# Token-major attention outputs, a dense output projection, a reordered opening and stacks copied on chip

## Chip, cores and metric

The kernel runs on one core of a Trainium2 chip. The metric is the device time of one execution, in microseconds, lower is better. The engines are named PE (TensorE), DVE (VectorE), ACT (ScalarE), POOL (GpSimd) and SP (SyncE, which here only issues DMAs). Each has its own in-order stream of instructions; they meet at semaphores that the program places by hand.

## What is computed

One transformer layer over 4 batches of 256 tokens with width 256, all in float32. Cut to what matters:

```python
h = layernorm(x)
q, k, v = rope(h @ Wq.T), rope(h @ Wk.T), h @ Wv.T          # then 16 heads of 16
kf, qf = elu(k) + 1, elu(q) + 1
mem_out = (qf @ (kf.T @ v)) / (qf @ kf.sum(tokens))         # linear attention
attn = softmax(q @ k.T / 4) @ v
g = sigmoid(gate)                                            # one number a head
x = x + (g * mem_out + (1 - g) * attn) @ Wo.T
u = layernorm(x)
x = x + fwht(silu(u @ W1.T) * (u @ W3.T)) @ W2.T             # fwht: Walsh-Hadamard over 1024
```

The transform fwht is applied once to W2 instead of to every token. W1 and W3 are 256 to 1024, W2 is 1024 to 256.

## The kernel before

**Precision.** Projections and the FFN split each operand into a high part (type F32R) and a low remainder, and add three products (hi-hi, hi-lo, lo-hi). `three` (L848 to L850), `ffn_up` (L1010, L1014) and `ffn_down` (L1032, L1036) do that.

**Attention scores.** For each head `q_stack` and `k_stack` (128 rows, one slot a head) hold three slots of 16 rows: q is (hi, lo, hi), k is (hi, hi, lo), so one matmul over all rows gives the split product. Rows 64 and 65 of q hold the negated row maximum (hi and lo), and those of k hold ones. So PE first computes all 16 heads' scores (`scores`, L901), DVE takes the row maxima (`row_maxima`, L628), the maxima are transposed, negated and sent by two small DMAs into rows 64 and 65 of `q_stack`, and PE computes the scores a second time, shifted and transposed (`shifted_scores`, L919). ACT takes the exponential (`exp_head`, L367), and `product_v` (L936) multiplies with v.

**Filling the stacks.** RoPE works on [feature, token] tiles: `rope_product` (DVE, L639), sums (`first_rope_sum`, L644, on DVE for batch 0; `rope_sums`, L506, on POOL after that), high part on ACT (`split_parts`, L325), low part (`first_low_part`, L649, DVE; `low_parts`, L513, POOL). SP writes the parts to a DRAM scratch `parts` (`write_parts`, L261), waits for that, and reads them back into the stacks (`load_stacks`, L274): for each half c of the heads six DMAs of 128 KB, each into 16 rows. For batches after the first they start when the shifted scores of the old half are done. The unused rows of both stacks are zeroed by POOL at the start (L490, L534, L536).

**Attention outputs before.** `product_v` leaves 4 heads at a time as [head strip of 32 rows, token], with the softmax denominator in row 16 of each strip. `read_memory` (L969) gives the linear part in the same layout. DVE's `weights` (L696 to L711) turns the denominators with 32x32 transposes, takes the reciprocal, multiplies by the gate and turns them back; `combine` (L720, L723) scales and adds. It is called in three pieces per batch: pieces 0 and 1 at the end of the batch's round, piece 2 early in the next round after head 2's row maxima. POOL's `norm_linear` (L531) scales the linear part. `project_out` (L988) then contracts the 128 strip rows of each of 4 groups with a `wo` that is half zeros, on top of the residual that `residual_in` (L979) brought in through the identity. `evac_x2` (ACT, L379) copies the sum to `xs`.

**Order of the work.** A prologue computes batch 0's q, k, v. Then rounds r = 0 to 4 are written out by hand for each engine. In round r PE computes the scores of batch r (16 heads), among them q, k, v of batch r + 1 and the output projection of batch r - 1; then 16 steps of shifted scores of batch r, among them the FFN chunks of batch r - 1 (8 chunks) and `product_v`. In every one of these steps h, PE takes what is listed for h in order, and a wait there holds all that comes later. The weight transform is done in between: `hadamard` (PE, L1046, in the prologue and at heads 6 and 7 of round 0), `butterfly` (L233; step 0 on POOL, steps 1 and 2 on DVE), `split_w2` and its low part. The low parts of W1 and W3 are two POOL instructions at L542.

**SP's queue** at the start: x of batch 0, Wq, Wk, x of batch 1, W1, W3; then, once the q, k, v weights are split, W2, x of batches 2 and 3, Wo. The DMAs of one queue are served in order.

## Time and profile before

| | us |
|---|---|
| median of 3 runs | 251.93 |
| lowest, highest | 249.94, 252.1 |
| the profiled execution, its own time | 254.45 |
| its span, first to last instruction | 252.6 |
| mean granted TensorE clock | 0.932 of full |

The page gives busy time by engine; the timeline gives start and duration of instructions, with the idle time before them and what ended it in brackets. A release by DMA means that the landing of that transfer was waited for.

### The profile page before, as it was taken

What the parts mean: (1) busy time and instruction counts of PE and PEld (TensorE: products, weight loads), DVE (VectorE), ACT (ScalarE), POOL (GpSimd) and SP (SyncE); (2) the same over time, 40 slices, a digit from 0 to 9 for tenths busy, and PEclk for the clock granted to TensorE, in tenths of its full rate; (3) what the DMA queues carried; (4) which work ended last, traced back from release to release, by engine and by line L of the source; (5) the groups of instructions that cost most, each with busy time, mean ns of one, the idle gap of its engine ahead of it and who ended that gap; (6) DMA issues with size and microseconds to landing.
All of it is one profiled execution on the core that took longest, in us unless ns stands there. A gap on an engine that the chain in (4) does not pass through costs nothing.

```text
span 252.6 us, 4048 instructions
## 1 busy us (share of the span) xinstructions
PE 200.2 (79%) x1444; PEld 169.1 (67%) x1444; DVE 174.9 (69%) x341; ACT 97.8 (39%) x196; POOL 95.7 (38%) x73
## 2 busy tenths in 40 slices
PE   0064066886897949999999699999879999959894
PEld 0064055873544939997788599877769986748893
DVE  6966862498898597838879967448998562962442
ACT  2261131042884012368810325686021577312231
POOL 7919500069450738323610492152021215111332
PEclk9999655799997997999999899999999999997999
DMA  6919299313087103002790130066800100000101
GB/s 217 384 29 260 86 176 120 38 43 130 0 122 114 22 31 111 31 2 51 79 128 1 43 114 20 4 91 99 109 0 0 49 0 3 1 1 0 44 0 42
DMA packets 16940, 17.67 MB, mean 70 GB/s; under 512 B 1676, under 2 KB 16268, under 8 KB 16908
## 3 DMA queue, kind: packets, MB, share of 16 engines
q1 hardware_dynamic: 16168, 16.68, 31.9%
q10 hardware_dynamic: 752, 0.73, 0.9%
q8 instruction: 11, 0.18, 0.4%
q14 instruction: 9, 0.07, 0.1%
HBM read 11.93 MB, written 5.24 MB: 68 GB/s over the span
## 4 chain that ended last, share of the span: by engine, by line
PE 43%; issue 22%; DVE 17%; POOL 8%; DMA 6%; SPq 2%; ACT 2%; POOLq 0%; DVEq 0%; ACTq 0%
DVE rowmax_pad L628 5%; DMA k_stack<-parts 5%; PE score_bank L901 5%; PE score_bank L1010 4%; PE exp_bank L919 4%; DVE xn L611 4%; PE down_bank L1032 4%; POOL hid_lo L525 4%; PE exp_bank L1010 3%; PE misc_bank L848 2%; DVE prod L639 2%; PE pv_bank L936 2%; PE misc_bank L849 2%; PE misc_bank L850 2%; PE misc_bank L969 2%
## 5 line engine op out<-in xcount | busy, mean ns | idle before, releaser
L628 DVE TENSOR_REDUCE rowmax_pad<-score_bank 128x2 f32<-128x512 f32 x64 | 42.8, 685 | 17.8 <-PE score_bank L901 17.8
L525 POOL TENSOR_TENSOR hid_lo<-wide_raw,hid_hi 128x256 fp32r<-128x256 f32 x32 | 25.0, 782 | 70.6 <-ACT hid_hi L400 67.1
L367 ACT ACTIVATE prob<-exp_bank 128x512 f32<-128x512 f32 x64 | 37.8, 601 | 15.4 <-PE exp_bank L919 15.1
L901 PE MATMUL score_bank<-k_stack,q_stack 128*128 128x256 f32 x128 | 31.1, 337 | 14.7 <-DVE rowmax_pad L628 10.5
L901 PEld LDWEIGHTS score_bank<-k_stack,q_stack 128*128 128x128 f32 x128 | 21.8, 205 | 20.0 <-DVE rowmax_pad L628 10.8
L919 PE MATMUL exp_bank<-q_stack,k_stack 128*128 128x256 f32 x128 | 28.5, 306 | 2.5 <-DMA q_stack<-nmT_lo 1.4
L919 PEld LDWEIGHTS exp_bank<-q_stack,k_stack 128*128 128x128 f32 x128 | 19.2, 189 | 14.0 <-issue 8.2
L506 POOL TENSOR_TENSOR roped<-prod 128x512 f32<-128x512 f32 x6 | 7.6, 1271 | 44.0 <-DVE prod L639 44.0
L738 DVE SCALAR_TENSOR_TENSOR wide_raw<-wide_raw,score_bank 128x256 f32<-128x256 f32 x16 | 6.7, 418 | 23.3 <-ACT wide_raw L394 23.3
L861 PE MATMUL misc_bank<-cst,xn 128*128 128x128 f32 x16 | 3.4, 351 | 23.9 <-DVE xn L611 23.9
L1032 PE MATMUL down_bank<-w_hi,hid_hi 128*128 128x256 f32 x64 | 17.5, 296 | 1.4 <-ACT hid_hi L400 1.4
L861 PEld LDWEIGHTS misc_bank<-cst,xn 128*128 128x128 f32 x16 | 2.3, 178 | 24.1 <-issue 13.1
L988 PE MATMUL pv_bank<-wo,att 128*128 128x256 f32 x64 | 16.3, 382 | 1.7 <-DVE att L723 1.7
L611 DVE TENSOR_SCALAR xn<-xs,mv,rstd 128x256 f32<-128x256 f32 x16 | 12.3, 809 | 7.6 <-POOL rstd L499 7.3
L1010 PE MATMUL exp_bank<-h2T_hi,w_hi 128*128 128x256 f32 x64 | 17.4, 294 | 0.0
L1010 PE MATMUL exp_bank<-h2T_hi,w_lo 128*128 128x256 f32 x64 | 17.1, 288 | 0.0
L1010 PE MATMUL score_bank<-h2T_hi,w_hi 128*128 128x256 f32 x64 | 17.0, 289 | 0.0
L1032 PE MATMUL down_bank<-w_lo,hid_hi 128*128 128x256 f32 x64 | 16.5, 281 | 0.0
L1010 PE MATMUL score_bank<-h2T_hi,w_lo 128*128 128x256 f32 x64 | 16.4, 280 | 0.0
L379 ACT ACTIVATE xs<-pv_bank 128x512 f32<-128x512 f32 x4 | 2.4, 598 | 35.1 <-DVE stats L592 35.1
L325 ACT ACTIVATE part_hi<-roped 128x512 fp32r<-128x512 f32 x8 | 5.0, 630 | 27.8 <-POOL roped L506 20.3
L936 PE MATMUL pv_bank<-prob,v_strips 128*32 128x256 f32 x192 | 15.3, 391 | 0.1
(117 smaller groups left out, 547.4 us busy)
## 6 DMA issues: line engine op xcount, KB each, us to landing
q_stack<-parts SPq DMA_DIRECT2D x24, 128.0 KB
k_stack<-parts SPq DMA_DIRECT2D x24, 128.0 KB
parts<-part_hi SPq DMA_DIRECT2D x8, 256.0 KB, 2.2
parts<-part_lo SPq DMA_DIRECT2D x8, 256.0 KB, 2.4
xs<-in_x SPq DMA_DIRECT2D x4, 256.0 KB, 6.6
wide_raw<-in_w1T SPq DMA_DIRECT2D x1, 1024.0 KB, 8.2
wide_raw<-in_w3T SPq DMA_DIRECT2D x1, 1024.0 KB, 10.0
narrow_raw<-in_w2T SPq DMA_DIRECT2D x1, 1024.0 KB, 6.0
```

The lines of the kernel that those rows point to most:

```text
L367: act.activation(prob[:, h % 8], exp_bank[h % 2][:], ACT.Exp, scale=SCALE).then_inc(prob_s, 1)
L506: pool.tensor_tensor(roped[:, c], prod[:, 2 * c], prod[:, 2 * c + 1], (ALU.subtract, ALU.add)[c]).then_inc(rope_sum, 1)
L525: pool.tensor_tensor(hid_lo[:, n % 3, :], ffn_work[n % 3], hid_hi[:, n % 3, :].bitcast(F32), ALU.subtract).then_inc(hid_lo_s, 1)
L611: dve.tensor_scalar(xn[:, tt, :], xs[:, b, tt, :], mv[:, tt, 0:1], rstd[:, tt:tt + 1], ALU.subtract, ALU.mult).then_inc(ln_xn, 1)
L628: dve.tensor_reduce(rowmax[:, h, :], score_bank[h % 2][:], AX.X, ALU.max).then_inc(rowmax_s, 1)
L738: dve.scalar_tensor_tensor(out=work, in0=work, scalar=1.0, in1=chunk_bank(n)[:, 0, :], op0=ALU.add, op1=ALU.mult).then_inc(gated_s, 1)
L901: mm = pe.matmul(bank[:, tt, :], q_stack[:, h, tt * P:tt * P + P], k_stack[:, h, :], start=True, stop=True)
L919: mm = pe.matmul(bank[:, tt, :], k_stack[:, h, tt * P:tt * P + P], q_stack[:, h, :], start=True, stop=True)
L936: mm = pe.matmul(bank[STRIP * j:STRIP * j + STRIP, half, :], v_strips[b % 2][:, tt, h, :], prob[:, h % 8, tt, :], start=(tt == 0), stop=(t ...
L988: mm = pe.matmul(bank[:, tt, :], att[:, g, tt * P:tt * P + P], wo[:, g, :], start=False, stop=(g == NG - 1), skip_group_check=True)
L1010: pe.matmul(bank[:, m, :], w[:, m, k, cols], h2T_hi[:, k, :], start=(k == 0 and w is w13_hi), stop=False)
L1032: pe.matmul(bank[:, tt, :], hid_hi[:, n % 3, tt * P:tt * P + P], w[:, c, :], start=(c == 0 and tt == 0 and w is w2_hi), stop=False, skip_g ...
```

## The change

1. **Opening.** POOL no longer clears the stacks. It fills a small tile with zeros and ones, and SP issues three DMAs that copy it into the rows the scores need (48 to 65 of q, 48 to 63 and 64 to 65 of k) behind W1. The scores contract 66 rows instead of 128. W3, W2, x of batch 2, Wo, x of batch 3 are issued only behind batch 0's twelve stack copies. ACT splits W1 and W3 after the work of batch 0. The low parts of W1 and W3 are cut into four POOL instructions each; W3's stand in round 0 ahead of butterfly step 0. All four hadamards stand at heads 5 to 8 of round 0. Batch 1's layer norm is ahead of batch 0's RoPE.
2. **Stacks.** `write_parts` and the DRAM scratch go. The columns of Wq and Wk are reordered on the host so that a half's 128 rows are (dim, head), and `load_stacks` copies straight from `part_hi` and `part_lo` in SBUF: four copies when the high part is ready, two when the low part is.
3. **Outputs.** `product_v` writes two groups into `pv_bank`; ACT copies them (`evac_att`); PE transposes them to [token, strip] (`transpose_att`, 4 transposes); DVE's `combine` takes the reciprocal of the denominators (now a column), multiplies by the gate, scales and adds the linear part, which `linear_part` has scaled straight from PSUM; PE transposes the 128 combined columns back (`transpose_comb`, 2 transposes), ACT copies them (`evac_combT`), and `project_out` contracts 2 x 128 dense rows. The residual is added by DVE at the head of `ln_statistics`. `residual_in`, `evac_lin`, `evac_x2` and `norm_linear` go. `read_memory` now streams 136 columns instead of 256.

```diff
 load_stacks(b, c):
-                sp.wait_ge(parts_out[c], 32 * (b + 1))
                 if b == 0:
-                    sp.wait_ge(stack_zero, 2)
+                    sp.wait_ge(stack_zero, 48)
                 else:
                     sp.wait_ge(exp_ps, NH * (b - 1) + HH * (c + 1))
...
+                for src, ready, slots in ((part_hi, part_hi_s, ((0, 0), (0, 2), (1, 0), (1, 1))),
+                                          (part_lo, part_lo_s, ((0, 1), (1, 2)))):
+                    sp.wait_ge(ready, DC * b + c + 1)
+                    for m, s in slots:
+                        sp.dma_start((q_stack, k_stack)[m][HD * s:HD * s + HD, HH * c:HH * c + HH, :].bitcast(F32),
+                                     src[:, c, m, :].bitcast(F32)).then_inc(stack_in[c], 16)

+            def late_loads():
+                sp.dma_start(wide_raw[:, 1], w3T.rearrange("(c p) n -> p c n", p=P)).then_inc(w13_in[1], 16)
...
+                sp.dma_start(w2_raw, w2T.rearrange("(c p) n -> p c n", p=P)).then_inc(w2_in, 16)
+                sp.dma_start(xs[:, 2], xv(x, 2)).then_inc(x_in[2], 16)
+                sp.dma_start(wo[:], woT.rearrange("(c p) n -> p c n", p=P)).then_inc(wo_in, 16)
+                sp.dma_start(xs[:, 3], xv(x, 3)).then_inc(x_in[3], 16)

 POOL, round 0:
                 if has(r + 1):
                     low_parts(r + 1)
                 if r == 0:
+                    wide_low(1)
                     butterfly(pool, 0)

 DVE:
+            def combine(b, u):
+                n = 2 * b + u
+                strips = pv_bank[:].rearrange("p t (s e) -> p (t s) e", e=STRIP)
+                dve.wait_ge(attT_ps, n + 1)
...
+                dve.reciprocal(att_inv[:]..., strips[:, :, HD]).then_inc(att_inv_s, 1)
+                dve.tensor_tensor(att_wt[:], att_inv[:], gate2[...]..., ALU.mult).then_inc(att_wt_s, 1)
+                dve.tensor_tensor(att_n[:]..., strips[:, :, 0:HD], att_wt[:]..., ALU.mult).then_inc(att_n_s, 1)
...
+                dve.tensor_tensor(comb[:, :, cols], att_n[:], lin_n[:, :, cols], ALU.add).then_inc(comb_s, 1)

 DVE, end of a round:
                 if has(r):
                     combine(r, 0)
                 if has(r + 1):
-                    row_maxima(r + 1, (0,))
+                    row_maxima(r + 1, (0, 1))
+                    memory_strips(r + 1)
                 if has(r):
                     combine(r, 1)

 PE, scores of round r:
-                    if h in (6, 7) and r == 0:
-                        hadamard(h - 4)
-                    if h == 0 and has(r - 1):
-                        residual_in(r - 1)
-                    if 1 <= h < 5 and has(r - 1):
-                        project_out(r - 1, h - 1)
+                    if h in (5, 6, 7, 8) and r == 0:
+                        hadamard(h - 5)
+                    if h == 1 and has(r - 1):
+                        transpose_comb(r - 1, 1)
+                    if h == 3 and has(r - 1):
+                        project_out(r - 1)

 PE, shifted scores of round r:
-                    if has(r) and h >= 5 and h % 4 in (1, 2):
-                        product_v(r, h // 4 - 1, h % 4 - 1)
+                    if has(r) and h in (5, 9):
+                        product_v(r, h // 4 - 1)
+                    if has(r) and h == 11:
+                        transpose_att(r, 0)
+                    if has(r) and h == 14:
+                        transpose_comb(r, 0)
...
                 ffn_down(chunk(r - 1, 5))
+                if has(r):
+                    product_v(r, 2)
+                    product_v(r, 3)
                 if has(r + 1):
                     scores(r + 1, (0, 1))
+                    memory(r + 1)
...
+                    transpose_att(r, 1)
                 ffn_down(chunk(r - 1, 6))
```

In the DVE stream `ln_normalise` of the second layer norm moves from head 5 to head 6, and `linear_part` stands after FFN gate 2. In the ACT stream `evac_att(r, 0)` stands at step 10, `evac_combT(r, 0)` at step 14, and `evac_combT(r - 1, 1)` at the head of the next round.

## Rows read from the trace of the kernel before

**Rows 1.** The page: busy time, share of the span, instructions
```profile
PE 200.2 (79%) x1444; PEld 169.1 (67%) x1444; DVE 174.9 (69%) x341; ACT 97.8 (39%) x196; POOL 95.7 (38%) x73
```
**Rows 2.** Busy time by stage: stage, length, engines, PE clock, DMA share, GB/s
```profile
0.00:41.60 41.60, 13.16 (x56) 10.85 (x57) 28.38 (x38) 12.65 (x16) 22.45 (x13) 0.82 0.69 186
41.60:63.50 21.90, 17.50 (x93) 15.00 (x93) 16.00 (x29) 4.29 (x8) 10.93 (x7) 0.87 0.39 76
63.50:99.40 35.90, 28.88 (x195) 21.50 (x196) 30.12 (x55) 15.94 (x27) 15.91 (x9) 0.90 0.35 55
99.40:129.40 30.00, 29.92 (x264) 25.52 (x263) 21.03 (x45) 18.43 (x40) 12.39 (x11) 1.00 0.38 69
129.40:147.60 18.20, 15.62 (x98) 14.19 (x98) 15.78 (x35) 3.52 (x7) 5.33 (x6) 0.91 0.23 34
```
**Rows 3.** Timeline of the opening: start, us, engine, line, operation [idle before]
```profile
5.68 3.51 POOL L534 MEMSET k_stack<- 128x4096 f32 x1
5.78 7.16 DVE L611 TENSOR_SCALAR xn<-xs,mv,rstd 128x256 f32<-128x256 f32 x2 [0.88 <-POOL rstd L499]
7.56 1.15 ACT L313 ACTIVATE wqkv_hi<-narrow_raw 128x512 fp32r<-128x512 f32 x2 [0.81 <-DMA narrow_raw<-in_wkT]
15.63 0.55 PE L848 MATMUL misc_bank<-hT_hi,wqkv_hi 128*128 128x256 f32 x1 [1.46 <-ACT hT_hi L319]
...
22.17 2.45 DVE L644 TENSOR_TENSOR roped<-prod 128x512 f32<-128x512 f32 x1
25.31 4.21 DVE L649 TENSOR_TENSOR part_lo<-roped,part_hi 128x512 fp32r<-128x512 f32 x1
30.16 0.69 DVE L644 TENSOR_TENSOR roped<-prod 128x512 f32<-128x512 f32 x1
...
32.73 1.41 SPq L274 DMA_DIRECT2D q_stack<-parts  x3
41.60 1.23 PE L901 MATMUL score_bank<-k_stack,q_stack 128*128 128x256 f32 x4 [2.22 <-DMA k_stack<-parts]
```
**Rows 4.** DMA rate from 28 to 50 us in 40 slices; loads, us to landing
```profile
GB/s 0 0 0 0 177 300 0 0 311 346 302 252 151 192 114 151 102 106 102 147 112 147 101 110 99 149 117 145 102 104 99 151 93 39 0 0 0 0 0 0
...
wide_raw<-in_w3T SPq DMA_DIRECT2D x1, 1024.0 KB, 10.0
narrow_raw<-in_w2T SPq DMA_DIRECT2D x1, 1024.0 KB, 6.0
```
**Rows 5.** Timeline of round 0
```profile
49.10 0.74 PE L901 MATMUL score_bank<-k_stack,q_stack 128*128 128x256 f32 x4
57.57 4.67 POOL L233 TENSOR_TENSOR wide_raw<-narrow_raw 128x1024 f32<-128x1024 f32 x2
62.21 2.77 POOL L517 TENSOR_SCALAR prod<-roped 128x1024 f32<-128x1024 f32 x1
67.47 1.05 ACT L338 ACTIVATE prod<-prod 128x1024 f32<-128x1024 f32 x1
77.73 0.85 PE L901 MATMUL score_bank<-k_stack,q_stack 128*128 128x256 f32 x4 [1.80 <-DMA k_stack<-parts]
```
**Rows 6.** Groups by line: busy us, mean ns of one, idle before
```profile
L711 DVE STREAM_TRANSPOSE narrow_raw<-ginv 128x256 f32<-128x256 f32 (+2 forms) x16 | 11.4, 712 | 0.6
L988 PE MATMUL pv_bank<-wo,att 128*128 128x256 f32 x64 | 16.3, 382 | 1.7 <-DVE att L723 1.7
L542 POOL TENSOR_TENSOR w_lo<-wide_raw,w_hi 128x2048 fp32r<-128x2048 f32 x2 | 9.5, 4766 | 0.0
L969 PE MATMUL misc_bank<-feat,mem 128*128 128x256 f32 x32 | 7.6, 380 | 0.0
L723 DVE TENSOR_TENSOR att<-att,wide_raw 128x256 f32<-128x256 f32 (+1 forms) x12 | 7.4, 617 | 0.4
```
**Rows 7.** Timeline of round 1: FFN gate 6 on DVE, step 14 on PE
```profile
123.57 0.42 DVE L741 TENSOR_TENSOR wide_raw<-wide_raw,score_bank 128x256 f32<-128x256 f32 x1
123.55 0.50 PE L919 MATMUL exp_bank<-q_stack,k_stack 128*128 128x256 f32 x2
```

More of the change, by code:

```diff
@@ L287, in _ @@
             for r in ROUNDS:
-                if has(r + 1):
-                    for c in range(DC):
-                        write_parts(r + 1, c)
                 if has(r):
@@ L299, in _ @@
             sp.wait_ge(y_out, 16 * TT * NB)
-            for c in range(DC):
-                sp.wait_ge(parts_out[c], 32 * NB)
         @block.scalar
@@ L432, in _ @@
                 if r == 0:
-                    evac_hadamard(2)
-                    evac_hadamard(3)
+                    for u in range(4):
+                        evac_hadamard(u)
                 if has(r - 2):
@@ L469, in _ @@
                         evac_hT(r + 2)
-                    if h == 11 and has(r):
+                    if h == 10 and has(r):
                         evac_att(r, 0)
+                    if h == 14 and has(r):
+                        evac_combT(r, 0)
                     if h == 15 and has(r - 1):
@@ L489, in _ @@
             pool.memset(mhalf[:], -0.5).then_inc(mhalf_set, 1)
-            pool.memset(q_stack[:].bitcast(F32), 0.0).then_inc(stack_zero, 1)
+            for k in range(2):
+                pool.memset(fill[:, k, :], float(k)).then_inc(fill_set, 1)
             def ln_power(n):
@@ L562, in _ @@
                         ln_power(LN[(1, r + 2)])
-                    if c == 4 and has(r):
-                        norm_linear(r)
                 if r == 0:
@@ L711, in weights @@
-                dve.transpose(rden[:, cols].rearrange("p (k n) -> p k n", n=STRIP),
-                              ginv[:, groups].rearrange("p g k -> p (g k)").unsqueeze(2).broadcast_to(full)).then_inc(rden_s, 1)
-            def combine(b, u):
-                weights(b, u + 1)
-                dve.wait_ge(rden_s, (NP + 1) * b + u + 2)
-                gs = PIECES[u]
-                piece = att[:, gs, :].rearrange("p g n -> p (g n)")
-                dve.tensor_tensor(piece, piece, rden[:, gs.start * S:gs.stop * S], ALU.mult).then_inc(norm_att, 1)
-                dve.wait_ge(norm_att, NP * b + u + 1)
-                dve.wait_ge(norm_lin, b + 1)
-                dve.tensor_tensor(piece, piece, lin[:, gs, :].rearrange("p g n -> p (g n)"), ALU.add).then_inc(comb_s, 1)
+                    dve.wait_ge(att_n_s, n)
@@ L784, in _ @@
                         row_maxima(r, (h,))
-                    if h == 2 and has(r - 1):
-                        combine(r - 1, 2)
                     if 3 <= h < 7 and has(r + 1):
@@ L792, in _ @@
                         ffn_gate(chunk(r - 2, 7))
-                    if h == 5 and has(r - 1):
+                    if h == 6 and has(r - 1):
                         ln_normalise(LN[(2, r - 1)])
@@ L814, in _ @@
                 ffn_gate(chunk(r - 1, 4))
-                if has(r):
-                    weights(r, 0)
                 if has(r + 1):
```

348 lines of the change are left out of this document (169 added, 179 removed).

## The prediction

> **What bounds the kernel now.** I read the page first: PE is busy for 79% of the span and DVE for 69% [rows 1], which names no single limit. So I cut the span at the first scores (41.6 us), the first shifted scores (63.5), the first FFN chunk of round 1 (99.4), the end of its last `ffn_down` (129.4) and the first FFN chunk of round 2 (147.6), and read the busy time in each [rows 2]. The reader should see three kinds of stage. From 99.4 to 129.4 PE is busy for 29.92 of 30.00 us at full clock: only PE's work, or a new wait on PE, counts there. From 129.4 to 147.6 DVE is busy for 15.78 of 18.20 us while PE waits: row maxima, the last piece of `combine`, RoPE products and a layer norm stand in one DVE queue. From 0 to 41.6 no compute engine is full (PE 13.16, DVE 28.38) and the DMA engines have 0.69: a chain of latencies. Then I read the timeline of the opening for that chain [rows 3] and the DMA rate under it [rows 4].
>
> **1. Opening, up to the first scores (now 41.6).** Two DVE instructions of the layer norm take 7.16 us, from 5.78 to 12.94, beside POOL's two clears of `k_stack` [rows 3]; they should take under 1. With the clears gone xn is there at about 6.6. Next late are the weights: the high parts of Wk and Wv run to 8.7 [rows 3], then ACT's copy of hT (0.6, estimate from its like) and DVE's low part (0.7): the projections start at about 10.0 instead of 15.63, -5.6. In the RoPE block a sum takes 2.45 and a low part 4.21 beside the low parts of W1 and W3 on POOL, where the same sum takes 0.69 a little later [rows 3]; POOL's work is now behind it: -(2.45 - 0.69) - (4.21 - 0.69) = -5.3. The stack DMAs now need no trip through DRAM and no second half: the first is issued when the first high part is ready, about 18.0, where the old one waits until 32.73. From first issue to first scores it took 41.60 - 32.73 = 8.9 [rows 3], and I keep that: 27.0. So **-14.6**. The fill DMAs (576 KB in all) stand behind W1 and have to land before 18; at the rate found below they take 3 to 6 us, which puts them between 16 and 20, so up to +2 lies in the range.
>
> **The price of an on-chip copy** is shown nowhere. While the twelve reads from DRAM run, the rate stays near 100 to 150 GB/s for about 12 us, 1.57 MB; just before, the parts went out of all 128 rows at 311 and 346 [rows 4]. So 1.0 us per 128 KB copy. Both kinds write 1 KB runs into 16 rows; only the source changes. Lower end 0.46 us, the time SP takes to issue one (1.41 for three [rows 3]); upper end three times today's, 3.0, since reads and writes now both fall on SBUF. I take 1.0, because the writes are the same.
> The Trainium skill (SBUF — State Buffer, "Door 1: The DMA port swizzle") says that rows 0 to 15 lie on 4 of 16 ports and gives 104 GB/s for such a transfer; by that rule the destination binds, the trace's 100 to 150 agrees, and the copies get no faster by leaving DRAM. If the source had bound, they would fall to the issue price and the time would be that of rival A.
>
> **2. Scores of round 0 (now 21.9).** W3 and W2 now queue behind twelve copies: these start at 18.6 and end near 31; 2 MB more follow. W2 alone took 6.0 from issue to landing and W3 behind W1 10.0 [rows 4]; I take 9.0 for both, so W2 lands at 40. PE wants it at head 5. Today heads 4 and 5 are through at 49.8 [rows 5], 8.2 after the first scores, so now at 35.2, and PE, in order, stands until 40: +4.8. DVE, waiting for scores, can't make it up, since it has one maximum a head to take. Two more hadamards of four matmuls each with an evacuation between, half of them at the lower clock (granted 0.87 here [rows 2]) add 1.4. **+6.2.** First shifted scores at 55.1 instead of 63.5.
>
> **3. From there to round 1's first FFN chunk (now 35.9).** POOL now does W3's low part in this round (4.8 [rows 6]) ahead of butterfly step 0 (4.67) and the minimum for elu (2.77) [rows 5]; both were waiting for the same last high part. ACT's exp for elu stands at step 5, at 67.47 [rows 5], 2.5 after POOL's minimum ends (64.98). POOL's 4.8 is one part made up, since the hadamards free it later for both: +1.4 of wait on ACT. Against that the wait of 1.80 for a stack DMA ahead of batch 1's first scores [rows 5] goes, because `product_v` for groups 2 and 3 now stands before them: -1.8. And the stretch of row maxima, as in step 4: -3.4. **-3.8.**
>
> **4. Start of rounds 1 and 2 (18.2 in the second).** DVE sets the pace. `combine` and `weights` for one piece are three transposes and scales; L711 alone is 11.4 us in 16, L723 7.4 in 12 [rows 6], and a piece of 256 columns adds up to six operations, 2.3 us. The new `combine` is two small operations and two of 256 columns: 1.4. Piece 1 saves 0.9; piece 2 (2.3) leaves the head of the round and 0.7 comes in for the residual: -1.6. About 0.9 of DVE's 2.4 idle in the stage [rows 2] closes, since project_out now has one wait instead of three. -3.4 in the round.
> What the end of the previous round adds is the **new wait at step 14**: PE's `transpose_comb(r, 0)` needs `combine(r, 0)`, and that stands in DVE's queue behind FFN gate 6, which ends at 123.99, while step 14's scores are issued at 123.55 [rows 7]. Without `product_v` of group 2 and with `transpose_att` PE comes there at 123.4; combine is done at 124.0 + 1.4 = 125.4. PE stands 1.8 to 2.0, and behind it wait step 15, ACT's exp 15 and the last FFN and `product_v`. PE's work in the stage moves little: `read_memory` has 1.9 us a batch (7.6 in 4 [rows 6]) and streams half: -0.6; ten of the twelve small transposes cost 0.9. Sum +2.2. Between its bounds (0, if the late FFN work hides it; 3, if ACT's queue adds) I take 2.2.
> The output projection itself, 4.1 us a batch (16.3 in 4 [rows 6]), halves, but stands where PE waits for DVE: nothing.
> Round 1 to 2: 2.2 - 3.4 = **-1.2**. Round 2 to 3 has no RoPE and so less wait to close: 2.2 - 2.7 = **-0.5**. Round 3 to 4: the chain from the last exp to the second layer norm is a transpose, a combine, a transpose, a copy, a projection, one after another; what DVE saves they take: **+0.3**.
>
> **Sum:** -14.6 + 6.2 - 3.8 - 1.2 - 0.5 + 0.3 = -13.6. The execution profiled took 254.45 with a span of 252.6, so 1.85 lie around the span, and 240.9 would be its own time. The median of the runs, 251.93, is 2.5 lower; the difference is carried over to it: 251.93 - 13.6 = **238.3 us**.
>
> **Rivals.**
> A. *W2 is there in time.* If the copies run at 0.5 instead of 1.0 us, the first scores come 3 us earlier and the queue ahead of W2 is 6 us shorter: the wait of 4.8 goes, and 238.3 - 3.0 - 4.8 = 230.5, less some of step 3: 229.5. For it: nothing of DRAM is left. Against: the rate was low with 16 target rows only. 0.20.
> B. *The wait at step 14 costs nothing.* FFN chunks 5 and 6 and two groups of `product_v` stand behind it, but PE is in order and full at 29.92 of 30.00 [rows 2]; only if DVE reaches gate 6 early. 238.3 - 3 x 1.9 = 232.6. 0.12.
> C. *The lighter start gives nothing back.* PE's own work with latencies fills the stage (15.62 of 18.20 [rows 2], some at the lower clock), and the extra trips PE, DVE, PE, ACT, PE stand in a row: 3.4 + 3.4 + 2.7 are lost: 247.8. 0.14.
> D. *Slower.* The on-chip copy is dear. Place: stack copies in the opening and at each round. At p us per copy W2 and first scores shift by 12 (p - 1.0), and batch 1, 2, 3's first scores wait when 6 p + 2 exceeds the about 12 us from the release of the half to them, 3 (6 p - 10). At p = 2.0: 12 + 6 = 18, over the 13.6 saved; it turns slower at about 1.8. At 2.0: 256.3. Against: writes bind today. 0.05.
> E. *The change's opening isn't what the chain sees*: the fills land late, at 20, and the projections wait for a constant or weight: +5, 243.5. 0.10.
> My forecast keeps 0.39.
>
> **How the numbers follow.** A measurement tells about 1% from no change, 249.4 to 254.4. Faster by more: all but D and a corner of C, 0.92; within 1%: 0.04; slower: 0.04. Range 229.0 to 247.5: it reaches to A and C.
>
> **What would show it.** xn under 1 us before 7 us; first scores near 27; a gap on PE before the first hadamard of 3 to 6 us ending when W2 lands; a wait of PE on DVE at the `transpose_comb` of each of rounds 1 to 3 of about 2 us; 33 us or less from the first shifted scores to round 1's first FFN chunk; about 16 us from the end of `ffn_down` 6 to the next round's first FFN chunk. It would be wrong if copies of 128 KB took more than 1.3 or less than 0.8 us, or if PE never stood at step 14.

## The result: 7.4% slower, and the profile after

The changed kernel takes 270.32 us (median of 4 runs, 269.53 to 271.07) beside 252.01 of the kernel before in the same session; the ratio is 1.0744, interval 1.0678 to 1.081. The forecast was 238.3, with 247.5 as its upper end. The profiled execution took 271.07, its span is 269.3. Medians are of all runs of a kernel, while a ratio and its 95% interval leave out the runs more than 1.5% above the kernel's fastest.

The page of the changed kernel: busy time, and TensorE's granted clock in 40 slices.
```profile
PE 201.0 (75%) x1444; PEld 173.6 (64%) x1444; DVE 145.4 (54%) x300; ACT 93.8 (35%) x188; POOL 72.7 (27%) x73
PEclk9995595955559575999999599999999999797999
```
The same clock row of the kernel before.
```profile
PEclk9999655799997997999999899999999999997999
```
VectorE and GpSimd shed 30 and 23 us of work, as the change set out to do, and TensorE's busy time is what it was [rows 1]. The time got longer without work: in waits, and in a clock that stands at its lower level (1.2 GHz, 0.50) in many slices between 29 and 107 us where before it was mostly full.

By stage (columns as in [rows 2]): up to the first scores, up to the first shifted scores, and from there to the first FFN chunk of round 1 in two parts; the last row goes from the end of round 1's last `ffn_down` to the first FFN chunk of round 2.
```profile
0.00:29.10 29.10, 8.52 (x49) 7.40 (x49) 17.22 (x37) 9.55 (x13) 7.10 (x13) 0.83 0.79 150
29.10:58.60 29.50, 20.08 (x101) 17.70 (x101) 15.13 (x25) 6.20 (x9) 11.82 (x9) 0.73 0.53 118
58.60:80.00 21.40, 19.70 (x110) 12.81 (x110) 11.96 (x19) 11.70 (x21) 6.59 (x4) 0.50 0.44 57
80.00:106.80 26.80, 17.64 (x88) 15.89 (x85) 19.38 (x30) 4.64 (x6) 12.25 (x7) 0.69 0.17 16
...
139.40:156.80 17.40, 13.90 (x86) 13.00 (x86) 13.59 (x26) 3.40 (x7) 6.13 (x6) 0.80 0.16 17
```
The stages of the runs. Each number is the time up to the start of the matmul named at the head, from the one named before it: the first is that of the first scores from the span's start, the last goes from round 4's first FFN chunk to the end. `e_best_b` and `e_open_best` are not in the table, since their traces caught one of their longest executions (257.60 and 257.96 us). The experiments are explained below.
```
                 scores shifted  FFN r1  FFN r2  FFN r3  FFN r4    end
before            41.6   22.0    35.8    48.2    42.5    39.1     23.4
forecast, change -14.6   +6.2    -3.8    -1.2    -0.5    +0.3       -
after             29.1   29.5    48.2    50.0    45.2    44.2     23.1
measured change  -12.5   +7.5   +12.4    +1.8    +2.7    +5.0     -0.3
e_open_only       28.8   31.5    40.8    48.7    44.0    38.9     22.3
e_out_only        40.8   21.1    43.3    49.6    45.2    45.5     22.4
e_w2_early        39.3   22.9    48.6    50.0    45.2    45.5     22.3
e_warm            28.8   29.4    39.3    51.4    45.1    42.5     22.3
e_w2lo_cut        28.8   30.2    40.4    50.4    47.1    45.5     22.3
e_out_mend        28.2   30.0    49.4    49.8    43.2    41.0     22.2
e_all_mends       28.3   29.6    40.8    49.6    43.2    41.0     22.2
e_open_warm       28.2   32.0    39.9    48.4    43.9    39.2     23.4
e_had_late        28.6   26.5    46.2    49.7    45.1    45.5     22.2
e_best_a          28.9   26.2    40.2    48.8    43.3    42.8     23.0
e_open_had        30.0   26.0    40.4    48.7    43.9    38.9     22.3
e_before_warm     46.1   21.9    35.8    48.1    42.4    39.1     23.3
e_out_cut         40.9   19.2    35.5    50.2    45.1    42.4     23.5
e_out_mended      40.9   20.8    35.9    48.4    43.2    41.1     23.4
```
The largest miss is the third column. Its place is seen in the timeline of the changed kernel around 83 us, on VectorE, GpSimd and TensorE (start, us, engine, line, operation, idle before). `att_wt` is the gated weight of each head, `att_n` the scaled attention output, `wide_raw` written by L715 the memory of `comb`, and `w_lo` the low part of W2:
```profile
82.50 0.25 DVE L698 RECIPROCAL att_inv<-pv_bank 128x16 f32<-128x16 f32 x1
82.79 4.42 DVE L702 TENSOR_TENSOR att_wt<-att_inv,gate 128x16 f32<-128x16 f32 x1
87.70 0.42 DVE L715 TENSOR_TENSOR wide_raw<-att_n,wide_raw 128x256 f32<-128x256 f32 x1
...
82.67 4.52 POOL L564 TENSOR_TENSOR w_lo<-wide_raw,w_hi 128x2048 fp32r<-128x2048 f32 x1 [17.47 <-ACT w_hi L425]
...
88.19 0.69 PE L939 MATMUL pv_bank<-cst,wide_raw 128*128 128x128 f32 x2 [4.31 <-DVE wide_raw L715]
```
A product of 16 columns takes 4.42 us. It starts 0.12 after GpSimd's low part of W2 and ends with it: 82.79 + 4.42 = 87.21, 82.67 + 4.52 = 87.19. `combine(0, 1)` is late by as much, and TensorE, at head 1 of round 1, stands 4.31 us before the transposes of `comb`. From there to 94 us the granted clock is 0.50, and from 100 to 106.8 again.

The opening, by contrast, went nearly as forecast. The last two rows are SyncE's wait ahead of the first copy and its place in the chain that ended last:
```profile
5.81 0.73 DVE L609 TENSOR_SCALAR xn<-xs,mv,rstd 128x256 f32<-128x256 f32 x2 [0.88 <-POOL rstd L500]
9.59 0.55 PE L836 MATMUL misc_pair<-hT_hi,wqkv_hi 128*128 128x256 f32 x1 [1.82 <-ACT hT_hi L332]
19.42 1.25 SPq L290 DMA_DIRECT2D q_stack<-part_hi  x2
29.09 1.22 PE L889 MATMUL score_bank<-k_stack,q_stack 66*128 66x256 f32 x4 [4.15 <-DMA k_stack<-part_lo]
42.98 2.08 PE L1041 MATMUL exp_bank<-narrow_raw,cst 128*128 128x256 f32 x4 [6.55 <-DMA narrow_raw<-in_w2T]
...
SPq L290 <- DMA k_stack<-fill: 2.6, 1, 2.6
5.10 14.31 DMA k_stack<-fill
```
The first high part was ready at 16.71 (ACT's copy at 16.08 took 0.63), earlier than forecast, but the fills landed at 19.41, and the first copy waited for them.

The DMA rate from 27 to 44 us in 40 slices: the copies to 36, at about 105 GB/s, then the loads at 340 to 425.
```profile
GB/s 142 106 104 96 96 101 99 108 94 104 96 109 140 99 101 104 111 157 145 106 270 405 424 395 405 386 361 340 349 349 354 347 347 352 352 342 352 246 22 24
```
One copy of 128 KB is thus 131 KB / 105 GB/s = 1.25 us, not 1.0; the twelve took from about 20.6 to 35.5 us. And the later rounds: what VectorE waited for before its row maxima (a group of the page), what TensorE waited for in all (us, times, longest), and one instance each.
```profile
L626 DVE TENSOR_REDUCE rowmax_pad<-score_bank 128x2 f32<-128x512 f32 x64 | 42.8, 686 | 46.0 <-PE score_bank L889 46.0
...
PE pv_bank L939 <- DVE wide_raw L715: 12.0, 6, 4.3
PE down_bank L1027 <- DVE xs L739: 3.9, 2, 2.0
...
130.97 0.42 DVE L733 TENSOR_TENSOR wide_raw<-wide_raw,score_bank 128x256 f32<-128x256 f32 x1
132.50 0.43 DVE L715 TENSOR_TENSOR wide_raw<-att_n,wide_raw 128x256 f32<-128x256 f32 x1
132.98 0.44 PE L939 MATMUL pv_bank<-cst,wide_raw 128*128 128x128 f32 x2 [2.21 <-DVE wide_raw L715]
...
167.11 0.35 PE L1027 MATMUL down_bank<-w_hi,hid_hi 128*128 128x256 f32 x1 [1.97 <-DVE xs L739]
```
The wait at step 14 is there as foreseen (2.21 behind gate 6 and `combine`, the successors of [rows 7]). The second was not foreseen: `second_residual` now stands behind `linear_part`, and the first `ffn_down` claims the bank that it reads.

### The profile page after: what moved, and what is told of

It is laid out like the page before. It is cut to its first block, busy times and chain, and to the rows that moved or that the text cites. A ratio compares the mean times of both kernels' runs of the same rounds, so it can differ in the third digit from the quotient of the medians.

```text
span 269.3 us, 3949 instructions
## 1 busy us (share of the span) xinstructions
PE 201.0 (75%) x1444; PEld 173.6 (64%) x1444; DVE 145.4 (54%) x300; ACT 93.8 (35%) x188; POOL 72.7 (27%) x73
## 4 chain that ended last, share of the span: by engine, by line
PE 33%; issue 27%; DMA 11%; DVE 11%; POOL 10%; SPq 4%; ACT 1%; POOLq 0%; DVEq 0%; ACTq 0%
DMA narrow_raw<-in_w2T 6%; DMA k_stack<-fill 5%; PE score_bank L889 4%; POOL hid_lo L526 4%; PE pv_bank L921 3%; PE down_bank L1027 3%; PE exp_bank L1005 3%; SPq L290 3%; PE exp_bank L907 3%; DVE rowmax_pad L626 2%; PE score_bank L1005 2%; PE exp_bank L1041 2%; POOL w_lo L537 2%; DVE att_wt L702 2%; PE pv_bank L984 2%
## 5 line engine op out<-in xcount | busy, mean ns | idle before, releaser
L889 PE MATMUL score_bank<-k_stack,q_stack 66*128 66x256 f32 x128 | 31.5, 346 | 13.4 <-DVE rowmax_pad L626 9.1
L889 PEld LDWEIGHTS score_bank<-k_stack,q_stack 66*128 66x128 f32 x128 | 22.8, 221 | 18.5 <-DVE rowmax_pad L626 10.9
L907 PE MATMUL exp_bank<-q_stack,k_stack 66*128 66x256 f32 x128 | 29.3, 338 | 2.1 <-DMA q_stack<-nmT_lo 1.4
L907 PEld LDWEIGHTS exp_bank<-q_stack,k_stack 66*128 66x128 f32 x128 | 21.8, 222 | 7.5 <-ACT prob L372 4.9
L399 ACT ACTIVATE wide_raw<-exp_bank 128x256 f32<-128x256 f32 x16 | 6.2, 385 | 31.6 <-PE exp_bank L1009 29.7
L1027 PEld LDWEIGHTS down_bank<-w_hi,hid_hi 128*128 128x128 f32 x64 | 12.3, 192 | 6.3 <-issue 4.3
L405 ACT ACTIVATE hid_hi<-wide_raw 128x256 fp32r<-128x256 f32 x32 | 13.3, 415 | 5.3 <-DVE wide_raw L733 5.0
L500 POOL TENSOR_TENSOR rstd<-var_eps,mhalf 128x2 f32<-128x2 f32 x8 | 6.0, 747 | 30.8 <-DVE var_eps L599 30.8
L1005 PEld LDWEIGHTS exp_bank<-h2T_hi,w_hi 128*128 128x128 f32 x64 | 13.1, 205 | 0.2 <-DVE wide_raw L733 0.2
L1009 PE MATMUL exp_bank<-h2T_lo,w_hi 128*128 128x256 f32 x64 | 13.2, 290 | 0.0
```

Source lines behind the costliest of these rows:

```text
L405: act.activation(hid_hi[:, n % 3, :], ffn_work[n % 3], ACT.Copy).then_inc(hid_hi_s, 1)
L889: mm = pe.matmul(bank[:, tt, :], q_stack[0:MAXROW + 2, h, tt * P:tt * P + P], k_stack[0:MAXROW + 2, h, :], start=True, stop=True)
L907: mm = pe.matmul(bank[:, tt, :], k_stack[0:MAXROW + 2, h, tt * P:tt * P + P], q_stack[0:MAXROW + 2, h, :], start=True, stop=True)
L1005: pe.matmul(bank[:, m, :], w[:, m, k, cols], h2T_hi[:, k, :], start=(k == 0 and w is w13_hi), stop=False)
L1009: mm = pe.matmul(bank[:, m, :], w13_hi[:, m, k, cols], h2T_lo[:, k, :], start=False, stop=(k == DC - 1))
L1027: pe.matmul(bank[:, tt, :], hid_hi[:, n % 3, tt * P:tt * P + P], w[:, c, :], start=(c == 0 and tt == 0 and w is w2_hi), stop=False, skip_g ...
```

## The experiments

The theory after the result: four causes, (T1) the half clock of round 0, (T2) VectorE standing beside GpSimd's uncut low part of W2 (the lock, for short), (T3) the order of the loads, and (T4) TensorE's in-order waits in the output path. The rivals are that one of them is all of it, or that a wait only moves.

### The two halves of the change

**e_open_only** is the kernel before with the change's opening, fills, stack copies, split low parts and late W3 and W2, and its own output path. **e_out_only** is the changed kernel with the old opening and the stacks through DRAM.

> The kernel before with the change's opening and on-chip stacks alone (late W3 and W2, stack copies, split low parts), and the old output path. Theory (the loss has two halves: the opening's load order leaves TensorE waiting for W2 and at half clock, and the new output path adds waits in every round): first scores at about 29, first shifted scores at 57 to 59, half clock through most of round 0's exps, round 1's first FFN chunk near 97 to 103, and rounds 1 to 4 as before or a little under; total 248 to 256. Rival (the opening alone is the whole loss): total above 262. Rival (the opening is a gain and the output path the whole loss): total 238 to 243, with the 12.5 us of the opening kept to the end.

> The changed kernel with the old opening, the stacks through DRAM and W2 early, and the new output path. Theory of two halves: the stages up to the first shifted scores as before (63.6), round 0's exps at full clock, then some 2 to 5 us lost per round to the in-order waits (step 14, attention transposes, down bank): total 258 to 264. Rival (the opening is the whole loss): total 250 to 254. Rival (the output path is the whole loss): total at or above 268.

Measured: e_open_only 256.75 us, ratio 1.0158 (1.0108 to 1.0208); e_out_only 268.95, ratio 1.0622 (1.0575 to 1.0669). The opening saves 12.8 and gives back 9.5 in the scores and 4.9 in the next stage; it is not a gain at all by itself. Its total is 0.75 above the range of my theory. The output path alone costs 16, above what I expected (258 to 264): the total lies in the range of the rival that it is the whole loss (268 or more), though the opening adds 3.9 of its own. In the trace of e_out_only the same thing stands, one operation further on:
```profile
82.03 0.18 DVE L699 TENSOR_TENSOR att_wt<-att_inv,gate 128x16 f32<-128x16 f32 x1
82.24 0.42 DVE L704 TENSOR_TENSOR att_n<-pv_bank,att_wt 128x256 f32<-128x256 f32 x1
82.70 4.31 DVE L712 TENSOR_TENSOR wide_raw<-att_n,wide_raw 128x256 f32<-128x256 f32 x1
...
82.22 4.51 POOL L561 TENSOR_TENSOR w_lo<-wide_raw,w_hi 128x2048 fp32r<-128x2048 f32 x1 [17.23 <-ACT w_hi L425]
...
87.06 0.69 PE L936 MATMUL pv_bank<-cst,wide_raw 128*128 128x128 f32 x2 [3.96 <-DVE wide_raw L712]
```
The product that reads `pv_bank` (PSUM) and one SBUF tensor runs its 0.42 us beside GpSimd's instruction; the sum of two SBUF tensors stands until it ends.

### The low part of W2 in pieces

```diff
-                    pool.tensor_tensor(w2_lo[:], w2_b, w2_hi[:].bitcast(F32), ALU.subtract).then_inc(w2_lo_s, 1)
+                    for k in range(FC):
+                        pool.tensor_tensor(w2_lo[:, k], w2_b[:, k], w2_hi[:, k].bitcast(F32), ALU.subtract).then_inc(w2_lo_s, 1)
```
**e_w2lo_cut** does this in the changed kernel, **e_out_cut** in e_out_only.

> The changed kernel with GpSimd's low part of W2 cut into 8 instructions. Theory (VectorE's 0.1 us product took 4.4 us because it stood behind the uncut 4.5 us instruction on GpSimd, and TensorE stood 4.3 us at the late transposes): that product under 0.8 us, the wait at the late transposes under 1 us, round 1's first FFN chunk 3 to 4.5 us earlier, total 265.5 to 267.5. Rival (the product waits for something else, or TensorE's next wait takes its place): the stage within 1 us of 48.2, total 269 to 271.

> The new output path on the old opening, with GpSimd's low part of W2 in 8 pieces. Theory (in the stage from first shifted scores to round 1's first FFN chunk the new output path loses by the lock at the combination alone, and by the clock that falls behind it): that stage 35 to 37.5 instead of 43.3, total 261 to 263. Rival (the lock is the opening's doing, or only one of several waits there): the stage at 40 or above, total 265 to 268.

Measured: 264.34 us, ratio 1.0468 (1.0374 to 1.0561), and 260.56, ratio 1.0312 (1.0261 to 1.0363). The stage falls from 48.2 to 40.4 and from 43.3 to 35.5, by 7.8 and 7.9; the medians of the whole fall by 6.0 and 8.4. The timeline of e_w2lo_cut:
```profile
82.11 0.25 DVE L699 RECIPROCAL att_inv<-pv_bank 128x16 f32<-128x16 f32 x1
82.39 0.18 DVE L703 TENSOR_TENSOR att_wt<-att_inv,gate 128x16 f32<-128x16 f32 x1
82.60 0.43 DVE L708 TENSOR_TENSOR att_n<-pv_bank,att_wt 128x256 f32<-128x256 f32 x1
83.06 0.53 DVE L716 TENSOR_TENSOR wide_raw<-att_n,wide_raw 128x256 f32<-128x256 f32 x1
...
82.57 5.76 POOL L565 TENSOR_TENSOR w_lo<-wide_raw,w_hi 128x256 fp32r<-128x256 f32 x8 [16.65 <-ACT w_hi L425]
```
GpSimd pays 5.76 instead of 4.52 us, VectorE 0.18 instead of 4.42. Not all of the 7.8 is the edit's. In e_w2lo_cut 0.8 and in e_out_cut 1.6 of it lie ahead of the reciprocal, where nothing had been changed (from the first shifted scores to it 23.9 and 23.1 us, 19.9 and 18.3). Behind it 7.0 and 6.3 come back. The stand of TensorE was 4.3 and 4.0 of that. The other 2 to 3 us go with less time at half clock (from the reciprocal to the FFN chunk the granted clock is 0.67 in the changed kernel and 0.81 in e_w2lo_cut, but 0.72 and 0.74 in the other pair); that they are the clock's is argued, not shown. On the old opening the stage is 35.5, and 35.9 in e_out_mended, which has the pieces too, beside 35.8 before: the output path loses nothing else there that these runs can tell.

### TensorE kept busy

**e_warm** adds matmuls, whose results nothing reads, into the down bank, idle in round 0, where the changed kernel's TensorE stands; **e_before_warm** and **e_open_warm** do so in the kernel before (where the 50 stand ahead of the first scores) and in e_open_only, both without the 30 of round 1.
```diff
+                    if h == 4 and r == 0:
+                        pe.wait_ge(v_sb, 1)
+                        filler(50)
+                    if 8 < h < NH and r == 0:
+                        filler(5)
+                    if h == 1 and r == 1:
+                        filler(30)
...
+                if r == 0:
+                    filler(20)
```

> The changed kernel with matmuls added in TensorE's idle time of round 0 and at round 1's second head (50 before the first Hadamard, 5 at each of heads 9 to 15, 20 at the end of the scores, 30 ahead of the late transposes), whose results nothing reads. Theory of the clock: with TensorE busy the granted clock stays at 1.0 from 36 to 90 us, the shifted scores and P times V of round 0 run in half the time, and the stage from first shifted scores to round 1's first FFN chunk falls from 48.2 to 38 to 42; total 260 to 264. Rival (the stage is set by waits, and the half clock is only their sign): the clock rises but the total moves by less than 2 us, 268.5 to 272.

> The kernel before with matmuls added in TensorE's idle time (50 ahead of round 0's first scores, 5 at each of heads 9 to 15, 20 behind the scores), whose results nothing reads. Theory (the kernel before loses little to the clock in round 0, where its rows show it full from 48 to 76 us; the half clock there belongs to the change): the first scores' block at 41.6 to 46 us runs faster by 1 to 2 us, the rest is unchanged or slower by as much: total 251 to 254. Rival (every version gains from a warm TensorE, so the gain of 9.8 us that the changed kernel had from it says nothing of the change): 244 to 249.

> The kernel before with the change's opening and on-chip stacks and the old output path, and matmuls added in TensorE's idle time of round 0 (50 before the first Hadamard, 5 at each of heads 9 to 15, 20 at the end of the scores). Theory (the opening's 12.8 us are lost again mostly through the clock at half level in round 0): the stage from first shifted scores to round 1's first FFN chunk falls from 40.8 to 35 to 37, that of the scores from 31.5 to 30, total 249 to 252. Rival (the opening moves W2 and with it GpSimd's and VectorE's work, which sets these stages whatever the clock): total 255 to 257.

Measured: e_warm 260.55 us, ratio 1.0291 (1.0247 to 1.0335); e_before_warm 258.62, ratio 1.0254 (1.0208 to 1.03); e_open_warm 257.43, ratio 1.0196 (1.0115 to 1.0278). In e_warm the clock holds where it was 0.50 before, and the same work takes less time (by stretch, columns as above):
```profile
58.20:66.00 7.80, 6.11 (x57) 4.00 (x56) 7.14 (x11) 6.11 (x11) 5.22 (x3) 1.00 0.08 20
66.00:72.00 6.00, 4.78 (x30) 3.47 (x22) 3.48 (x7) 4.98 (x10) 0.00 (x0) 0.82 1.03 108
72.00:78.00 6.00, 6.00 (x63) 4.59 (x63) 2.87 (x8) 3.00 (x3) 0.89 (x1) 0.90 0.67 110
```
So 9.8 us of the changed kernel's 18 could be had back through the clock, 8.9 of them in the failed stage, though VectorE still stood 4.39 us beside GpSimd. The kernel before has nothing of the kind to win: its later stages stay within 0.15 us, and its first is 4.5 longer, by the 50 matmuls ahead of its scores (6.2 by the medians). In e_open_warm the matmuls were of no use: from 68 to 76 us the clock is at 0.50 all the same.

### Orders in the output path

**e_out_mend** is the changed kernel with `second_residual(r - 2)` ahead of `linear_part(r)` on VectorE, and:
```diff
-                    if has(r) and h == 14:
-                        transpose_comb(r, 0)
...
                     transpose_features(r + 1)
+                if has(r):
+                    transpose_comb(r, 0)
                 ffn_down(chunk(r - 1, 5))
```
**e_all_mends** has this, the pieces and e_warm's matmuls together; **e_out_mended** has this and the pieces on the old opening.

> The changed kernel with two orders mended: the second residual ahead of the linear part on VectorE, and the transposes of the first combined half from head 14 to behind the feature transposes. Theory (each in-order wait of about 2 us holds TensorE): rounds 1 to 3 shorter by 1.5 to 2 us each through the transposes, by 2 more in rounds 2 and 3 through the residual, and the last stage changes little; total 261 to 264. Rival (TensorE only meets the chain exps, P times V, transposes, combination later): waits at L931 and L939 grow in place of those removed, total 267 to 271.

> The changed kernel with the added matmuls in TensorE's idle time, the low part of W2 cut into 8, and both orders mended. Theory (clock, lock and in-order waits are separate losses and add up): 260.5 from the added matmuls, less 3 for the lock, less 5 to 7 for the orders: 250 to 254. Rival (they overlap: with the clock full the other waits are hidden, or the other way round): 256 to 260.

> The new output path on the old opening, with the low part of W2 in 8 pieces, the second residual ahead of the linear part, and the transposes of the first combined half behind the features' ones. Theory (the token-major outputs cost by their orders and by the lock alone): stages 40.8, 21, 36, 49, 43.2, 41, 22: total 252 to 256, the last two rounds still 1 to 2 us above the kernel before by the longer chain at the rounds' ends. Rival (with orders mended the dense output projection shows as a gain): 246 to 250.

Measured: 265.50 us, ratio 1.0525 (1.0447 to 1.0602); 257.24, ratio 1.0204 (1.0118 to 1.0289); 256.49, ratio 1.0162 (1.012 to 1.0204). In e_out_mend the wait at the moved transposes is 0.72 instead of 2.21, and that for the down bank is gone; yet the stage of round 2 gains only 0.2, those of rounds 3 and 4 gain 1.9 and 3.2, and that of round 1 is 1.2 longer. The two edits were made together; round 2's stage has the moved transposes without the moved residual (`second_residual` begins a round later), so there the wait of 2 us at step 14 was worth 0.2. The clock's, the lock's and the orders' gains add up to 9.8 + 6.0 + 4.8 = 20.6 if taken alone, and give 13.1 together. The failed stage is 39.3 with the added matmuls, 40.4 with the pieces and 40.8 with everything: the two remove the same time there. With everything mended on the old opening the output path still takes 4.0 us more than the kernel before by the medians, 1.2 by the two profiled spans (253.8 and 252.6; the profiled execution of before was 2.5 above its median); the stage before round 4's FFN, whose chain is longer by two transposes and a copy, has 2.0 more.

### The order of the loads

**e_w2_early** issues W3 and W2 behind W1 and the fills, ahead of the stack copies, and no longer in `late_loads` (those lines are not shown).
```diff
+            sp.dma_start(wide_raw[:, 1], w3T.rearrange("(c p) n -> p c n", p=P)).then_inc(w13_in[1], 16)
+            sp.wait_ge(wqkv_hi_s, 3)
+            sp.wait_ge(wqkv_lo_s, 3)
+            sp.dma_start(w2_raw, w2T.rearrange("(c p) n -> p c n", p=P)).then_inc(w2_in, 16)
+
             def late_loads():
```

> The changed kernel with W3 and W2 issued behind W1, ahead of the stack copies. Theory (W2's landing at 43 sets the first half of the loss): TensorE's wait of 6.5 us at the first Hadamard goes, first scores stay at 29 to 31, first shifted scores at 50 to 53 instead of 58.6, and with the clock less often at its lower level round 1's first FFN chunk at 92 to 98 instead of 106.8; total 256 to 262. Rival (the wait only moves: the Hadamard evacuations, GpSimd's low part of W3 and its butterfly are next, and the clock falls all the same): shifted scores at 56 or later, total 266 to 270.

Measured: 274.36 us, ratio 1.0837 (1.076 to 1.0913), if anything slower than the change itself (the two intervals overlap), and neither theory nor rival. W2 no longer makes TensorE wait, but the first scores come at 39.3. TensorE stands idle for the 10 us before them, while the queue is full:
```profile
29.10:39.30 10.20, 0.00 (x0) 0.00 (x0) 0.00 (x0) 0.00 (x0) 0.00 (x0) 0.50 1.16 117
```
The copies now share the queue with 2 MB more. My reading is that the sum of the transfers binds the opening. In the changed kernel the copies take 14.9 us and the fills about 7.5 behind W1 (11.9 to 19.4, the rate falling from 113 GB/s to under 40); these 22 us of the queue are needed in either order, and one order delays W2, the other the scores. That is an estimate, and it doesn't explain all: 2 MB at the 340 to 425 GB/s of the loads are some 6 us, but the scores come 10.2 later, and W2, issued at 10.11, landed only 23.0 later. No run leaves out the fills or makes them smaller.

**e_had_late** leaves the loads and moves the four Hadamard matmuls to heads 11 to 14, and their evacuations behind `evac_v(1)`.
```diff
-                    if h in (5, 6, 7, 8) and r == 0:
-                        hadamard(h - 5)
+                    if h in (11, 12, 13, 14) and r == 0:
+                        hadamard(h - 11)
```

> The changed kernel with the four Hadamard matmuls at heads 11 to 14 of round 0 instead of 5 to 8 (and their evacuations behind round 1's V on ScalarE). Theory (heads 5 to 15 of round 0 stand in order behind a W2 that lands at 43, and what waits on them would run in that time): the wait of 6.5 us at the first Hadamard falls under 2, first shifted scores at 51 to 54 instead of 58.6; the later stages keep at least half of it: total 262 to 267. Rival (the chain W2, Hadamard, GpSimd's low part and butterfly, VectorE's butterflies, W2's halves is what sets round 0's end): first shifted scores earlier, but round 1's first FFN chunk within 1 us of 106.8, total 269 to 272.

Measured: 265.10 us, from 260.31 to 266.15 in four runs beside 252.98. The shortest had a granted clock of 0.905 over the span, the others 0.867 or 0.868; with one run apart from three by 2% no ratio is given. The wait at the Hadamards is gone, shifted scores come at 55.1 instead of 58.6, and the FFN chunk at 101.2 instead of 106.8: the theory's direction. The total lies in its range, the shifted scores 1 us behind theirs.

### Putting it together

**e_best_a**: e_had_late, the pieces, both orders, and round 1's negative part on GpSimd ahead of W3's low part. **e_best_b**: the same with 5 added matmuls at each of heads 3 to 15, 20 behind the scores and 10 in round 1. **e_open_had**: e_open_only with late Hadamards, the negative part ahead and the pieces. **e_open_best**: that with 10, 24 and 24 added matmuls.

> The changed kernel with late Hadamards, round 1's negative part on GpSimd ahead of the low part of W3, the low part of W2 in 8 pieces, the residual ahead of the linear part and the late transposes behind the features' ones; no added matmuls. Theory (the change is slower only by the orders around it): first shifted scores at 51 to 54, the next stage 38 to 42, rounds 49.7, 43.2, 41.0, the end 23: total 247 to 252, below the kernel before's 252.8 by up to 2%. Rival (the clock at half level takes what the waits give back): 255 to 260.

> The same with matmuls added in round 0 (5 at each of heads 3 to 15, 20 behind the scores, 10 at round 1's second head), whose results nothing reads. Theory (the clock still falls in round 0 once the stalls are mended, and the added work keeps it up): 3 to 6 us under the version without them, 244 to 248. Rival (with the stalls gone the clock holds by itself and the added work only costs): equal or up to 3 us slower, 248 to 254.

> The kernel before with the change's opening and on-chip stacks, the old output path, late Hadamards, the negative part ahead and the low part of W2 in 8 pieces. Theory (the opening's gain was lost to the Hadamards in order and the half clock behind them): first shifted scores at 52 to 55 instead of 60.3, the next stage 36 to 40, total 245 to 250. Rival (the opening only moves the load of W2 and the rest follows it): total 254 to 257.

> The version with the change's opening, on-chip stacks, the old output path, late Hadamards, the negative part ahead and W2's low part in pieces, with matmuls added where its trace shows TensorE waiting ahead of the exps (10 at head 5, 6 at each of heads 12 to 15, 24 behind the scores). Theory (its shifted scores and P times V still run at half clock from 60 to 76 us, for want of work at 52 to 56): that stage 36 to 38 instead of 40.4, total 246 to 249. Rival (the added work delays the maxima as much as the clock gives): 250 to 253.

Measured: e_best_a 254.54 us, ratio 1.0108 (1.0064 to 1.0152); e_best_b 251.53, ratio 0.9967 (0.9925 to 1.001); e_open_had 251.01, ratio 0.994 (0.9894 to 0.9985); e_open_best 254.42, ratio 1.0003 (0.996 to 1.0045; six of its twelve runs, from 250.6 to 259.1 at a clock of 0.887 to 0.937, count for the ratio). All fell short of their theory, by 1.0 to 5.4 us. The version that is faster than both kernels is e_open_had, by 0.6%, with 0.9985 as the upper end of its interval: the opening and the stack copies kept, the output path left as it was. Of the 11.6 us that its opening saves, 4.0 go in the scores and 4.6 in the stage after. There its shifted scores and `product_v` run at half clock:
```profile
60.00:64.00 4.00, 4.00 (x26) 2.41 (x19) 3.80 (x6) 2.39 (x4) 0.00 (x0) 0.50 0.00 0
64.00:70.00 6.00, 5.74 (x32) 3.05 (x35) 4.67 (x7) 3.86 (x8) 3.25 (x1) 0.50 0.88 110
70.00:76.00 6.00, 6.00 (x40) 3.51 (x36) 4.05 (x10) 2.44 (x5) 0.00 (x0) 0.50 0.42 56
```
Why the clock does not come back in these 16 us, in which TensorE is shown busy for 15.7, while in the kernel before it is 0.90 over the whole stage [rows 2], stays open; the added matmuls did not settle it.

## Why the prediction was wrong

The step that failed is **3, "From there to round 1's first FFN chunk", -3.8**, measured +12.4. It can be taken apart with the runs. Old opening and new outputs, with W2's low part in pieces: 35.45 - 35.81 = -0.4. The uncut low part, that is VectorE's stand and what follows it: 43.31 - 35.45 = +7.9, of which 1.6 arose ahead of the edited instruction. The new opening, with the old outputs: 40.75 - 35.81 = +4.9. The three make 12.4. The first two rest on runs with and without one edit; what makes the 4.9 is open. So:
- The lighter start of the round (-3.4) gave back almost nothing here, as rival C had it: the wait of 1.80 for a stack DMA did go (batch 1's first scores at 80.05 stand behind none), and still the stage is only 0.4 shorter without the lock.
- I priced the new small operations by their columns (1.4 us for a `combine`) and did not ask what runs on GpSimd beside them. The trace of before shows the same stand, on a product of two SBUF tensors in the old `weights`, cheap there only because it began near the end:
```profile
72.50 3.27 POOL L531 TENSOR_TENSOR wide_raw<-wide_raw,narrow_raw 128x1024 f32<-128x1024 f32 x1 [6.46 <-DVE narrow_raw L711]
75.07 0.73 DVE L706 TENSOR_TENSOR ginv<-inv,gate 128x16 f32<-128x16 f32 x1
79.59 0.17 DVE L706 TENSOR_TENSOR ginv<-inv,gate 128x8 f32<-128x8 f32 x1
...
82.77 4.55 POOL L567 TENSOR_TENSOR w_lo<-wide_raw,w_hi 128x2048 fp32r<-128x2048 f32 x1 [7.01 <-ACT w_hi L420]
86.18 0.43 DVE L696 STREAM_TRANSPOSE narrow_raw<-att 128x256 f32<-128x256 f32 x1
86.89 0.46 DVE L706 TENSOR_TENSOR ginv<-inv,gate 128x8 f32<-128x8 f32 x1
```
  Both long ones end with GpSimd's instruction (75.80 and 75.77; 87.35 and 87.32); alone such a product takes 0.17. Beside the low part of W2 the old kernel had a row maximum, a transpose and a reciprocal, which passed, and the products of two SBUF tensors in its `weights` and `combine` came from 86.89 on, as GpSimd ended; the new `combine` has two such operations, and they came at its start, on the path to TensorE. I even used this effect in step 1, where such a sum took 2.45 instead of 0.69 [rows 3], and did not ask where it would be made anew.
  The Trainium skill has the rule (SBUF — State Buffer, "SBUF: two separate sides"): a VectorE operation with two SBUF inputs and a GpSimd operation that reads SBUF share one pair of ports, and whichever starts first keeps it for its whole instruction. The traces agree: the short products end within 0.03 us of GpSimd's instruction and the sum of 256 columns 0.3 behind it, and `att_n`, with one of its operands in PSUM, passes in 0.42.
- The clock: I carried a granted clock of about 0.9 over from the rows of before. It was 0.50 from 58.6 to 80.0 us, and adding matmuls gave 9.8 us back. I had forecast stops of TensorE (4.8 us before the first Hadamard) and did not ask what they do to the clock. No run ties the half clock to that stop, though: in e_had_late it is gone, and the clock is still 0.51 from 55 to 75 us.

**Step 1, -14.6**: measured -12.5. xn at 6.54 and the projections at 9.59 as said (6.6, 10.0). The first high part was there at 16.71 instead of 18.0, but the first copy was issued at 19.42, 2.6 us of waiting for the fills. Their landing lay inside the 16 to 20 that I had given them, but the sum had no term for it; rival E named the place. From the first issue to the first scores it took 9.7 instead of 8.9.

**The price of a copy, 1.0 us**: 1.25, inside the bounds. The copies got no faster by leaving DRAM, which is what a bound by the destination gives, as the row was read. W2 landed at 42.9 instead of 40: the copies started 2.0 later than the 18.6 of the forecast and took 14.9 instead of 12.4, and W3 and W2 took 7.4 behind them instead of 9.0. The mechanism of rival D was right, but what it shifts is 3 us, not 18. (238.3 + 5 of rival E is 243.3, not 243.5.)

**Step 2, +6.2**: +7.5. The gap before the first Hadamard is 6.55 instead of 4.8, by W2's landing. e_had_late shows that only 3.0 of the 7.5 go with it.

**Step 4**: the wait at step 14 has its forecast size (2.21, forecast 1.8 to 2.0), but in round 2's stage it is worth 0.2, near to rival B. The forecasts -1.2, -0.5 and +0.3 came out at +1.8, +2.7 and +5.0. Missed were the wait for the down bank (2 us in two rounds), the end of a round, where 2.0 stay in the last one with all orders mended (the longer chain, as I read it), and that a lighter VectorE gives TensorE nothing when VectorE is then found waiting for it: 46.0 us of idle time before its row maxima.

Of my signs, those on xn, the first scores, the gap (6.55 for 3 to 6) and the waits at `transpose_comb` came out nearly as written; the 16 us to the next round's FFN chunk were 17.4. Neither of the two that were to prove me wrong came. The one that failed was the stage of step 3, 48.2 instead of 33 or less.

My range ended at rival C. No rival had the output path itself as the slower side; runs give it 16 us alone.

## What to carry to other kernels

Before replacing a long operation by small ones, lay them over the other engine's timeline: an operation of 0.2 us with two SBUF inputs can stand as long as the longest uncut GpSimd instruction beside it, and what waits for it stands as well. Cut such GpSimd instructions into pieces (1.2 us more for eight pieces of a 4.5 us one bought 6 to 8 us here). And when an opening is shortened, add up what its transfers need of the queue at their own rates: if that sum binds, the gain is paid back where the displaced load is wanted, and look at the granted clock of the stage behind it (0.50 here for 21 us).

## What the runs showed of the hardware

- Pieces of GpSimd's subtraction, 8 of 256 columns, take 5.76 us where one of 2048 takes 4.52, and VectorE's short sums get between them with at most 0.1 us of delay (0.53 for 0.43).
- Copies inside SBUF into 16 rows run at about 105 GB/s, 1.25 us each; reads from DRAM into the same rows ran at 100 to 150, some 1.0 us each [rows 4]; loads over all 128 rows behind the copies at 340 to 425.
- A fill of two rows of `k_stack` by a copy of 32 KB was issued at 5.10 us, behind W1 and 544 KB of other fills, and landed at 19.41.
- The granted clock stayed at 0.50 from 58.6 to 80.0 us with TensorE shown busy for 19.70 of the 21.40. Busy time in the profile alone does not tell that the clock will be full.
- The granted clock of one kernel differs between its runs (0.887 to 0.937 in e_open_best); the two at 0.887 took 257.96 and 259.13 us, the one at 0.937 took 250.62.
